# State products on stacked halves, a second landing buffer for the first rows' weights, and new orders of work

## The reference, cut to what matters

```python
x = x + (einsum('bnh,boh->bno', x, W[subject]) + b[subject])          # L0: 512 x 512 weights per row
x = x + layernorm-with-gamma/beta(x + W2(relu(W1 x + b1)) + b2)       # L1: weights by language
x = x + L2(x)
x = x + zX * lap_x(x) + zY * lap_y(x) + zR * x * (1 - x)              # L3: neighbours in channel and time
```

```python
def L2(x):                                        # per row
    ctx = causal_ema(x, tau_ctx)
    gated = x * sigmoid([x, ctx] @ Wg + bg)
    mod = 0.5 + sigmoid(gelu(x @ Wn1 + bn1) @ Wn2 + bn2)        # T x 32
    traces[d] = causal_ema(gated * mod[:, d], tau[d])           # h = alpha_d * h + b, 32 of them
    temporal = sum_d softmax(blend)[d] * traces[d]
    gate = sigmoid(temporal @ Wtemp + btemp)
    soma = gelu(x @ Wsoma + bsoma)
    return layernorm((soma * gate) @ Wout) * gamma + beta
```

## Time and profile before

| | |
|---|---|
| median of 3 runs | 1044.95 us (1042.16 to 1045.16) |
| the profiled execution's own time | 1038.77 us |
| its span | 1037.0 us |
| PE, DVE, POOL, ACT busy | 919.3, 831.4, 615.0, 392.7 us |
| mean granted TensorE clock | 0.97 |

### The profile page before, as it was taken

One profiled execution on the slowest core, in us unless ns is written; L12 is line 12 of the kernel. 1 busy time (PEld: TensorE's weight loads), 2 busy tenths in 40 slices (PEclk: granted clock), 3 DMA queues, 4 the chain that ended last, 5 costly groups with the idle time before them and its releaser, 6 DMA issues.

```text
span 1037.0 us, 18886 instructions
## 1 busy us (share of the span) xinstructions
PE 919.3 (89%) x6088; PEld 776.7 (75%) x6088; DVE 831.4 (80%) x1333; ACT 392.7 (38%) x730; POOL 615.0 (59%) x654
## 2 busy tenths in 40 slices
PE   2678899999899999999999999999999999998961
PEld 1458697878778787878878787887878787887751
DVE  3788779797978979798888979698887969697762
ACT  3463433434243443434343342425343343424220
POOL 1445447484756668484766749475766748474523
PEclk9779999999999999999999999999999999999985
DMA  6664333534343343534454353434344353420011
GB/s 218 214 212 137 108 123 111 165 107 155 115 153 133 116 163 108 158 118 135 129 146 132 122 168 105 155 102 162 124 131 154 104 161 114 141 72 32 31 41 61
DMA packets 92815, 133.28 MB, mean 129 GB/s; under 512 B 15692, under 2 KB 32588, under 8 KB 92716
## 3 DMA queue, kind: packets, MB, share of 16 engines
q1 hardware_dynamic: 88372, 125.93, 38.9%
q10 hardware_dynamic: 4344, 6.14, 1.9%
HBM read 106.86 MB, written 8.39 MB: 111 GB/s over the span
## 4 chain that ended last, share of the span: by engine, by line
DVE 33%; issue 24%; POOL 19%; PE 16%; ACT 3%; DMA 2%; SPq 1%; ACTq 1%; POOLq 0%; DVEq 0%
PE bank L1241 6%; DVE work L998 5%; PE bank L1371 4%; DVE w_r L829 4%; POOL work L416 4%; POOL xh L391 3%; DVE work L1007 3%; POOL b_t L403 2%; PE bank L1233 2%; POOL work L452 2%; DVE work L1014 2%; DMA w_land<-in_L_cond_weight 2%; DVE amath L975 2%; DVE work L1068 2%; POOL work L457 2%
## 5 line engine op out<-in xcount | busy, mean ns | idle before, releaser
L416 POOL TENSOR_TENSOR work<-work 128x448 f32<-128x448 f32 (+3 forms) x224 | 200.3, 894 | 35.4 <-DVE work L998 18.5
L1241 PE MATMUL bank<-x2h,wg_r 128*128 128x256 f32 x1536 | 198.2, 284 | 12.8 <-DVE bank L946 12.8
L1241 PEld LDWEIGHTS bank<-x2h,wg_r 128*128 128x128 f32 x1536 | 185.8, 188 | 27.3 <-DVE bank L946 16.9
L1371 PE MATMUL bank<-gh,amath 128*128 128x512 f32 x384 | 106.1, 412 | 21.7 <-DVE work L998 17.2
L998 DVE TENSOR_TENSOR work<-bank,work 128x512 f32<-128x512 f32 (+7 forms) x256 | 105.1, 446 | 19.5 <-POOL work L416 14.0
L1233 PE MATMUL bank<-w_r,xh 128*128 128x512 f32 x384 | 106.2, 415 | 15.6 <-DVE w_r L829 11.3
L403 POOL TENSOR_TENSOR b_t<-b_t,work 128x512 f32<-128x512 f32 x32 | 51.8, 1618 | 107.9 <-DMA b_t<-in_L_cond_b 66.0
L1241 PE MATMUL bank<-x2h,wsoma_r 128*128 128x256 f32 x768 | 107.5, 289 | 3.7 <-ACT work L615 3.5
L1371 PEld LDWEIGHTS bank<-gh,amath 128*128 128x128 f32 x384 | 68.0, 190 | 55.6 <-DVE amath L975 16.3
L829 DVE TENSOR_TENSOR w_r<-w_land,w_r 128x1024 fp32r<-128x1024 f32 x64 | 85.5, 1337 | 26.6 <-ACT w_r L542 26.6
L1241 PEld LDWEIGHTS bank<-x2h,wsoma_r 128*128 128x128 f32 x768 | 94.4, 188 | 12.7 <-issue 7.2
(11 more groups left out here) (142 smaller groups left out, 1651.1 us busy)
## 6 DMA issues: line engine op xcount, KB each, us to landing
w_land<-in_L_cond_weight SPq DMA_DIRECT2D x64, 512.0 KB, 3.9
w_t<-in_L_cond_W SPq DMA_DIRECT2D x64, 256.0 KB, 3.2
work<-work SPq DMA_DIRECT2D x64, 224.0 KB, 2.5
work<-in_xT SPq DMA_DIRECT2D x32, 256.0 KB, 3.5
b_t<-in_L_cond_bias SPq DMA_DIRECT2D x32, 256.0 KB, 3.5
work<-in_x SPq DMA_DIRECT2D x32, 256.0 KB, 3.4
work<-in_L_cond_beta SPq DMA_DIRECT2D x32, 256.0 KB, 3.5
b_t<-in_L_cond_b SPq DMA_DIRECT2D x32, 256.0 KB, 3.3
```

The source lines that it names most:

```text
L416: g_.tensor_tensor(dst, dst, src, ALU.add).then_inc(S["acc_ready"], 1)
L1241: ins = mm(dst, weight[:, w_part, first_block + a, o * P:(o + 1) * P], act[:, x_part, a], start=(not onto and a + w_part + x_part == 0), s ...
L1371: ins = mm(STATES[r][s_][:, :], amath[:, a_part, s_ * P:(s_ + 1) * P], gh[:, g_part], start=(a_part + g_part == 0), stop=(a_part == 1))
```

## The change

**State products.** Time inside the chunk buffers is now ordered (h q k): two halves h of 64 steps, then q, then 8 chunks k. So the first 8 chunk states (s_ = 0 and 1) depend on time rows 0 to 63 only. For them the 128 rows of the array are shared: `amath[64:128, 0]` gets a copy of the high weights of rows 0 to 63 (`amat_dup`), and a third slot `gh[:, 2]` holds the high part of g's first 64 rows above the low part of the same rows (`g_top`, `g_bottom`). One matmul gives hi*hi + hi*lo, a second one of 64 rows gives lo*hi: two for three. Three ACT copies per row are new. `state_weights_lo` waits for `amat_dup`. Chunk terms and adds are cut in 8 pieces where there were 4, of half the length each.

**Landing.** For rows 0 to 2 the second half of the L0 weights lands in `spare_land`, a part of `x2b` that is free until pair 1 needs it; `x2_plus_beta` of pair 1 waits for that.

**Loads.** gamma2, beta2 (256 KB each, from ACT's queue) and zX, zY, zR (from the head of SP's) move to SP's step -1 (`late_constants`). Wn1 is sent for later. The transposed x goes out first, ahead of the wait for the indices.

**Buffers.** `m` shares `h1T`, and the gelu in `mod_hidden` waits for the readers of m.

**Orders.** All five loops are written anew.

```diff
-        STEPS = range(-5, NP + 1)
+        STEPS = range(-6, NP + 2)
+        SPARE_ROWS = 3
+        def landing(b, half):
+            if b < SPARE_ROWS:
+                return (spare_land, 2 * b) if half else (w0_land[:, :, :], max(0, 2 * b - 1))
+            return w0_land[:, :, :], 2 * b - 1 if (b == SPARE_ROWS and not half) else 2 * b + half
...
-        h1T, m_q = buf("h1T"), buf("m")
+        h1T = buf("h1T")
+        m_q = h1T
...
-        gh = sb("gh", [P, 2, C], f32r)
+        gh = sb("gh", [P, 3, C], f32r)
...
-                for dst, src in ((zraw[:, 0], zx), (zraw[:, 1], zy), (zraw[:, 2], zr)):
-                    sp.dma_start(dst, src.partition_broadcast(P)).then_inc(const2_loaded, 16)
-                sp.wait_ge(ids_loaded, 2 * 16)
+                def late_constants():
+                    sp.dma_start(beta2[:, :], l2_beta.partition_broadcast(P)).then_inc(beta2_loaded, 16)
+                    sp.dma_start(gamma2[:, :], l2_gamma.partition_broadcast(P)).then_inc(gamma2_loaded, 16)
+                    for dst, src in ((zraw[:, 0], zx), (zraw[:, 1], zy), (zraw[:, 2], zr)):
+                        sp.dma_start(dst, src.partition_broadcast(P)).then_inc(const2_loaded, 16)
...
-                    if half or b:
-                        sp.wait_ge(S["w0hi_ready"], 2 * b + half)
-                        sp.wait_ge(S["w0lo_ready"], 2 * b + half)
+                    land, n_free = landing(b, half)
+                    if n_free:
+                        sp.wait_ge(S["w0hi_ready"], n_free)
+                        sp.wait_ge(S["w0lo_ready"], n_free)
...
-                    width = NK * (Q - j)
-                    src = RING[n % 2][:, at_:at_ + 4 * width].rearrange("p (a r t) -> p a r t", a=2, r=2)
+                    width = KH * (Q - j)
+                    src = RING[n % 2][:, at_:at_ + 8 * width].rearrange("p (x t) -> p x t", x=8)
...
+            def g_top(p, r):
+                act.wait_ge(S["ghi_ready"], 2 * p + r + 1)
...
+                a_.activation(gh[0:P // 2, 2], gh[0:P // 2, 0].bitcast(f32), ACT.Copy).then_inc(S["gtop_ready"], 1)
+            def g_bottom(p, r):
+                act.wait_ge(S["glo_ready"], 2 * p + r + 1)
...
+                a_.activation(gh[P // 2:P, 2], gh[0:P // 2, 1].bitcast(f32), ACT.Copy).then_inc(S["gbottom_ready"], 1)
+            def amat_dup(p, r):
+                act.wait_ge(S["amathi_ready"], 2 * p + r + 1)
+                a_.activation(amath[P // 2:P, 0, 0:2 * P], amat[0:P // 2, 0:2 * P], ACT.Copy).then_inc(S["amatdup_ready"], 1)
...
-                for a_part, g_part in ((0, 0), (0, 1), (1, 0)):
-                    ins = mm(STATES[r][s_][:, :], amath[:, a_part, s_ * P:(s_ + 1) * P], gh[:, g_part],
-                             start=(a_part + g_part == 0), stop=(a_part == 1))
+                if s_ < 2:
+                    mm(STATES[r][s_][:, :], amath[:, 0, cols_], gh[:, 2], start=True, stop=False)
+                    ins = mm(STATES[r][s_][:, :], amath[0:P // 2, 1, cols_], gh[0:P // 2, 0], start=False, stop=True)
+                else:
+                    for a_part, g_part in ((0, 0), (0, 1), (1, 0)):
+                        ins = mm(STATES[r][s_][:, :], amath[:, a_part, cols_], gh[:, g_part],
+                                 start=(a_part + g_part == 0), stop=(a_part == 1))
```

More of the change, by code:

```diff
@@ L509, in _ @@
                     x2_plus_beta(i + 2, 1)
+                if live(i + 3):
+                    rstd(mv_a, rs_a, 1, i + 3, 0)
+                if live(i):
+                    neighbours(i, 1)
+                    row_neighbours(i, 1)
+                    quadratic(i, 1)
+                if live(i + 3):
+                    x_plus_b0(i + 3, 1)
+                    x_plus_beta(i + 3, 1)
+                    x1_plus_b2(i + 3, 1)
+                if live(i + 2):
+                    add_terms(i + 2, 2)
+                    add_terms(i + 2, 3)
+                    add_terms(i + 2, 4)
+                    add_terms(i + 2, 5)
+                if live(i + 1):
+                    rstd(mv_c, rs_c, 2, i + 1, 0)
+                if live(i + 2):
+                    add_terms(i + 2, 6)
+                    add_terms(i + 2, 7)
         @block.scalar
@@ L700, in _ @@
             for i in STEPS:
+                if live(i):
+                    amat_hi(i, 1)
+                    amat_dup(i, 1)
+                if live(i + 1):
+                    x2_turned(i + 1, 0)
+                if live(i):
+                    g_top(i, 1)
+                    g_bottom(i, 1)
+                if i == 1:
+                    act.wait_ge(zt_ready, 1)
+                if live(i - 1):
+                    slopes(i - 1, 0)
+                if live(i + 1):
+                    x2_hi(i + 1, 1)
@@ new lines, in _ @@
+                if live(i):
+                    tn_copy(i, 0)
+                if i == -1:
+                    vj_hi_parts(range(Q))
+                if live(i + 2):
+                    x_hi(i + 2, 1)
+                if i == -2:
+                    load_wn1()
+                if live(i + 1):
+                    x2_turned(i + 1, 1)
+                if live(i):
+                    tn_copy(i, 1)
+                if i == -2:
+                    hi_parts(0)
+                if live(i):
+                    t_hi(i, 0)
@@ new lines, in _ @@
+                if i == -1:
+                    hi_parts(3)
+                if live(i + 1):
+                    wg_tanh(i + 1, 0)
+                if live(i + 2):
+                    w0_hi(i + 2, 1, 1)
+                if i == -6:
+                    logs()
+                if live(i - 1):
+                    slopes(i - 1, 1)
+                if i == -2:
+                    next_matrix(2)
+                if live(i + 1):
+                    wg_tanh(i + 1, 1)
+                if i == -2:
+                    mod_weights()
@@ L828, in w0_lo @@
                 blocks = slice(half * CC // 2, (half + 1) * CC // 2)
-                v_.tensor_tensor(w0_r[:, 1, blocks], w0_land[:, :, :], w0_r[:, 0, blocks].bitcast(f32), ALU.subtract).then_inc(S["w0lo_ready"], 1)
+                v_.tensor_tensor(w0_r[:, 1, blocks], landing(b, half)[0], w0_r[:, 0, blocks].bitcast(f32), ALU.subtract).then_inc(S["w0lo_ready"], 1)
             def low_rows():
```

596 lines of the change are left out of this document (291 added, 305 removed).

## The result

The changed kernel takes 1057.28 us (median of four), the kernel before beside it 1043.56 us: a ratio of 1.0125, 95% interval [1.007, 1.018]. The kernel is slower, by 12 to 14 us, where I forecast 1004 us, 984 to 1030. The profiled execution took 1053.17 us against 1038.77.

A forecast was written before the change was run, and what follows sets the result against it. PE, busy for 95% of the steady part, has nearly no slack; short DVE and POOL chains make it wait. Savings 15.4 + 18 + 8 = 41.4 us off 1038.77 give 997.4; with 6.2 for the median, 1004 us, range 984 to 1030.

The forecast's parts named there:

- Stacked products: PE's state products: 64 matmuls fewer at 0.241 us each, 15.4 us saved, bounds 0 to 26.4.
- 64 rows at half a slot: Aside on state products: had a 64-row matmul cost half a slot, the saving would be 31 us.
- The new orders: Steady part: fewer waits for scans and chunk terms, net of copies 1.2 us a pair, 18 us, bounds 0 to 30.
- The copies: Three more ACT copies a row, ahead of row 1's products: charged 0.3 us a pair, 0 to 1.3.
- near 1 us: PE's idle ahead of row 1's first state product, said to stay at that size despite the copies.
- The start: First rows: second landing buffer and earlier loads cut PE's idle, 8 us gained, bounds 0 to 20.
- Pieces of 64 and the layout: Chunk terms and adds in twice the pieces: nothing charged, at most 3 us of DVE off the path.
- DVE and POOL hold the pace: Rival, steady part: shorter products only add PE idle; scans 13 and start 8 gained, 1024 us; chance 0.18.
- Slower: the copies become a wait: Rival: DVE passes delayed by POOL and one open copy cost 4 us a pair, 1064 us; chance 0.08.

The follow-up runs named there:

- d1: Changed kernel with four of POOL's additions a row done on 16 of 512 columns, the rest left out: 1007.42 us, ratio 0.9647.
- g2: Changed kernel with four POOL additions a row on 16 of 512 columns, three full matmuls for every product and no copies: 1002.83 us, ratio 0.9609.
- a2: Changed kernel with three full matmuls for every state product, without the three copies: 1060.98 us, ratio 1.0195.
- c3: Kernel before plus layout in halves, second landing buffer, shared `m` and early constants; old orders, three full matmuls, no copies: 1035.61 us, ratio 0.9932.
- f4: Changed kernel with three full matmuls, no copies, POOL's list from the kernel before and constants loaded early: 1061.08 us, ratio 1.0199.
- g3: c3 with four POOL additions a row on 16 of 512 columns: 990.62 us, ratio 0.9473.
- c2: c3 with stacked products, the second matmul over all 128 rows, and the three copies put into ACT's old list: 1068.68 us, ratio 1.0248.
- h1: Changed kernel with the four matmuls of the two stacked products grouped as 128, 128, 64, 64 rows: 1058.11 us, ratio 1.0191.
- a3: Changed kernel with the single landing buffer of before for all rows: 1073.32 us, ratio 1.0293.
- b1: Kernel before with the second landing buffer alone added: 1040.68 us, ratio 0.9996.
- a1: Changed kernel with the second stacked matmul over all 128 rows, `amat_dup` later in ACT's list: 1052.91 us, ratio 1.0099.
- g1: Changed kernel with four POOL additions a row on 16 of 512 columns and the second stacked matmul over all 128 rows: 1003.70 us, ratio 0.9607.

## Why the prediction was wrong

Two steps failed, the price of the new orders, which is the larger, and the price of a stacked product.

**Stacked products (15.4 us expected).** The step that failed: "I take it as one whole slot, as the full one." Alone it is one; behind and ahead of a matmul of another height each slot is 0.43 us. The term's true size in PE's work is -0.3 us x 32 rows, 10 us of loss. As time it is not resolved: d1 is 4.6 us slower than g2, and their intervals overlap. My bound below was zero, for no good reason but that a pass less cannot cost. The prediction's sentence on 64 rows at half a slot has a wrong sum as well: three slots would become one and a half in 64 places, 64 x 1.5 x 0.241 = 23 us and not 31.

**The new orders (18 us expected).** This is the larger miss: the sum took the waits that would vanish and put no price on where the moved passes would land. The scans' wait did vanish, and 31.9 us of DVE's wait for `quadratic` too. But DVE's idle time was filled by passes that lie on POOL's, 0.35 us (`final_sum`) to 0.9 us (`temporal_lo`) longer each, and a new wait on `temporal_lo` took 13.8 us. a2 against c3 is the orders alone, but for the place of the constants, which f4 clears: 25 us of loss where I forecast 18 + 4.5 of gain before the copies. Their first marks are at 107.44 and 108.46 us, a pair takes 59.86 and 58.70: 16 us of the loss lie in the steady part, the rest behind it. g3 against g2 says that half of it goes with POOL's work, and the waits say which: chunk terms and `temporal_lo`. For the other half the one long wait left is that for the turned x2; no run moved it, so this is read from the trace and not tested.

The sum also took the clock as fixed. The mean granted clock is 0.961 of 1051.4 us where it was 0.970 of 1037.0: that is 82 us at 1.2 GHz (twice 0.039 of the span) against 62. Twenty us more at half speed can cost up to 10 of the span's 14.4 us. Where rows were read, a low stretch begins behind idle time of PE (below), so it would be a part of what a wait costs and not a rival to it; no run holds the clock fixed, so its share is not shown.

**The copies (4.5 us).** In the new orders about right: PE waits for L1043 ahead of the first product 11.2 us in 12 pairs, 0.94 a pair, as "near 1 us". The 1.16 us for L975 from which I reckoned was the only wait of that kind between 250 and 850 us, not a usual one. In the old orders the same copies cost 33 us at least (c2 against c3), so the term depends on the lists around it.

**The start (8 us).** x1 of rows 0 and 1 did come sooner. DVE by time, before:

```profile
27.12 0.69 DVE L906 TENSOR_TENSOR work<-bank,work 128x512 f32<-128x512 f32 x1 [0.69 <-PE bank L1233]
45.27 0.69 DVE L906 TENSOR_TENSOR work<-bank,work 128x512 f32<-128x512 f32 x1 [0.53 <-PE bank L1233]
```

and after:

```profile
25.05 0.69 DVE L974 TENSOR_TENSOR work<-bank,work 128x512 f32<-128x512 f32 x1
39.73 0.69 DVE L974 TENSOR_TENSOR work<-bank,work 128x512 f32<-128x512 f32 x1 [2.47 <-POOL work L425]
```

2.1 and 5.5 us sooner (4 and 8 expected). But the first mark is 2.2 us late. The chain of after has this ahead of it:

```profile
59.79 9.88 DMA w_land<-in_L_cond_weight
```

ACT's list stands behind that landing, with a relu (L593) for which PE then waits 4.74 us. It is not the same in every execution: h1, which does the same up to the first product, has its first mark at 106.53 us, a2 at 107.44, the changed kernel at 115.56. So the start gives somewhere between 7 us and nothing, and my 8 is the upper end; what it gives in the median I can't say from single profiles. The medians say that the buffer is worth some 17 us in the new orders (a3) and nothing in the old ones (b1), a dependence that the prediction did not see.

**Pieces of 64 and the layout: nothing expected.** c3 bears it out: no slower.

**The rivals.** "DVE and POOL hold the pace" (0.18) had the right place, though not wholly: a1 against the changed kernel and g1 against g2 show that most of PE's saved work becomes waiting, a1 against a2 that some 8 us may come out. Its time, 1024, was wrong, as it kept the scans' gain and put no price on the collisions. "Slower: the copies become a wait" (0.08) had the right sign and the right rule, two-input passes of DVE against POOL, but the wrong passes: `x2_row` did grow by 0.69 us, yet with it `temporal_lo` and `final_sum`, which the new orders put there. And it weighed 0.08 with 1064 us and an `L975` at 1.81 us on the page.

## What to carry to other kernels

An order that removes waits is not priced until each moved pass of DVE with two SBUF inputs is laid beside what POOL does at that time; the gain is the waits that go minus those lengths, and in a kernel whose PE is busy for 95% of the time a shorter product gives little or nothing while chains of other engines set the pace. Be wary of mixed heights of matmuls in a stream: here each change of height cost 0.19 us, and full height or grouping avoids it. And try a change's parts in the old order first: here one part alone (c3, 1035.6 us) beat both kernels.
